# One-hots of a chunk as eight comparisons of 128 columns with a value per partition

## What is computed

```python
def gmm_conv(x, src, dst, edge_attr, g, mu, sigma, root_w, bias):      # K = 3 kernels
    diff = edge_attr[:, None, :] - mu[None, :, :]
    gauss = jnp.exp(jnp.sum(-0.5 * diff * diff / (EPS + sigma[None] ** 2), axis=-1))
    xj = x[src] @ g
    msg = jnp.einsum('eko,ek->eo', xj.reshape(E, K, OUT_DIM), gauss)
    summed = segment_sum(msg, dst)
    cnt = segment_sum(ones(E), dst)
    return summed / jnp.maximum(cnt, 1.0)[:, None] + x @ root_w + bias

x = layernorm(x + silu(gmm_conv(x, src, dst, ...) + x))
# two SAGE layers on the same edges: h @ W_self + mean_of_neighbours(h) @ W_neigh + b, relu between
x = layernorm(x + sage(relu(sage(x))))
```

## Time and profile before

| | us |
|---|---|
| median of 3 runs | 7659.32 (7652.49 to 7663.15) |
| the profiled execution's own time | 7651.4 |
| its span, first to last instruction | 7649.6 |
| DVE busy | 4374.6 (57%) |
| POOL busy | 3367.5 (44%) |
| PE busy | 5050.4 (66%) |
| L1329, 489 recorded, mean 1212 ns | 592.7 |

### The profile page before, as it was taken

The page is one execution under the profiler, slowest core; times in us unless marked ns, Lnnn a source line. Parts: engine busy times, 40 slices in busy tenths (PEclk is TensorE's granted clock), DMA queues, the critical chain, the costliest instruction groups (busy, mean ns, idle before and its releaser), DMA issues.

```text
span 7649.6 us, 144672 instructions
## 1 busy us (share of the span) xinstructions
PE 5050.4 (66%) x35195; PEld 4048.2 (53%) x35196; DVE 4374.6 (57%) x15088; ACT 2714.0 (35%) x8317; POOL 3367.5 (44%) x3146
## 2 busy tenths in 40 slices
PE   1565655555566666655555555555545899999999
PEld 1223333333344444444444444444425899999999
DVE  5668888767677777665656656566543322222222
ACT  3113333334444444455555555555532000000000
POOL 5024555555666666666666666666630000000000
PEclk9558888877788888777778888788775899999999
DMA  2001222212222222222222222222230799999998
GB/s 71 28 24 49 68 68 68 67 51 87 78 96 83 87 91 90 90 90 91 90 90 91 91 90 90 73 90 90 91 85 3 298 381 383 381 367 385 385 384 344
DMA packets 258352, 1082.32 MB, mean 141 GB/s; under 512 B 140102, under 2 KB 144230, under 8 KB 194406
## 3 DMA queue, kind: packets, MB, share of 16 engines
q1 hardware_dynamic: 142806, 968.66, 32.8%
q0 software_dynamic: 100352, 102.96, 6.9%
q10 hardware_dynamic: 14902, 8.11, 0.5%
HBM read 751.67 MB, written 327.81 MB: 141 GB/s over the span
## 4 chain that ended last, share of the span: by engine, by line
PE 39%; DVE 20%; issue 14%; DVEq 13%; POOL 5%; DMA 5%; ACT 4%; ACTq 1%; SPq 1%; POOLq 0%
PE pw L970 21%; PE pw L800 9%; DVE rE L1269 5%; POOL rE L512 5%; DVEq L1302 3%; DMA tab<-tab_d 3%; DVEq L1472 3%; PE pw L825 3%; DVE rE L1267 2%; DVE rE L1329 2%; PE pw L772 2%; ACT rE L559 1%; DVE rE L1395 1%; PE pw L937 1%; ACT sca L575 1%
## 5 line engine op out<-in xcount | busy, mean ns | idle before, releaser
L512 POOL DMA_INDIRECT rE<-in_x,idx x3136 | 3365.4, 1073 | 2262.7 <-issue 2092.9
L800 PE MATMUL pw<-rE 128*128 128x193 f32 x7824 | 1775.9, 391 | 921.5 <-DVE rE L1329 885.9
L598 ACT CAST rB<-pw 128x792 bf16<-128x792 f32 x1568 | 1259.6, 814 | 2903.6 <-PE pw L825 1489.4
L800 PEld LDWEIGHTS pw<-rE 128*128 128x128 f32 x7824 | 1623.7, 233 | 1130.5 <-DVE rE L1329 1061.5
L559 ACT ACTIVATE rE<-rE,cols 128x64 f32<-128x64 f32 x4704 | 1254.5, 344 | 8.2 <-DMA tab<-tab_d 8.2
L825 PE MATMUL pw<-rE 128*128 128x396 f16 x3840 | 804.1, 357 | 577.8 <-DVE rE L1269 576.8
L1269 DVE TENSOR_SCALAR rE<-iperm,gr 128x392 f16<-128x392 f16 x3840 | 1052.1, 314 | 0.0
L825 PEld LDWEIGHTS pw<-rE 128*128 128x128 f16 x3840 | 368.8, 103 | 954.4 <-DVE rE L1269 681.1
L970 PE MATMUL pw<-rB,rA 128*128 128x192 bf16 x9604 | 810.8, 246 | 0.1
L970 PE MATMUL pw<-rE,rA 128*128 128x192 bf16 x9604 | 810.4, 246 | 0.1
L970 PEld LDWEIGHTS pw<-rB,rA 128*128 128x128 bf16 x9604 | 790.8, 98 | 1.6
(11 more groups left out here) (256 smaller groups left out, 2626.6 us busy)
## 6 DMA issues: line engine op xcount, KB each, us to landing
rA<-count SPq DMA_DIRECT2D x392, 1568.0 KB, 8.5
count<-rB SPq DMA_DIRECT2D x98, 3136.0 KB
rE<-in_x,idx POOLq DMA_INDIRECT x3136
cols<-cols_d SPq DMA_DIRECT2D x98, 64.0 KB
cols_d<-rA SPq DMA_DIRECT2D x3, 1568.0 KB, 5.2
rA<-in_edge_attr ACTq DMA_DIRECT2D x1, 4608.0 KB
out<-gcol ACTq DMA_DIRECT2D x97, 32.0 KB, 5.8
count<-rB SPq DMA_DIRECT2D x8, 224.0 KB, 2.0
```

What stands on the lines that cost most here:

```text
L512: pool.indirect_dma_start(out=gath[:, s, u * CB + b, :], out_offset=None, in_=x, in_offset=bass.IndirectOffsetOnAxis(ap=idx[:, s, u * CB + ...
L598: act.copy(stage[:, s, :, j * 2 * W:(j + 1) * 2 * W].rearrange("p h (w n) -> p w h n", w=2), pu[j % 3][:, :, 0:CW].rearrange("p w (h n) -> ...
L800: ins = pe.matmul(sums[side][:, 0:AW], onehot[:, side, bb, :], wgath[:, side, bb, :], start=(bb == 0), stop=(bb == CB - 1))
```

## The change

The one instruction that writes the one-hots of all eight batches, comparing two operands of 128 x 1024 (the iota repeated for each batch, `local` repeated along the columns), becomes eight instructions. Each compares the 128 columns of `iota` with one column of `local`, taken as a value per partition. The last of the eight raises the semaphore. The bytes written, the waits and everything on the other engines are as before.

```diff
@@ -1326,9 +1326,9 @@
                     V.tensor_scalar(local[:], here[:, 0, :], tile128[:, bass.ds(tile, 1)], None, ALU.subtract).then_inc(a_loc, 1)
                     add_sums(k, side)
                     dve.wait_ge(a_loc, k)
-                    V.tensor_tensor(onehot[:, side], iota[:, None, :].broadcast_to([P, CB, P]),
-                                    local[:, :, None].broadcast_to([P, CB, P]),
-                                    ALU.is_equal).then_inc(a_oh[side], 1)
+                    for bb in range(CB):
+                        ins = V.tensor_scalar(onehot[:, side, bb, :], iota[:], local[:, bb:bb + 1], None, ALU.is_equal)
+                    ins.then_inc(a_oh[side], 1)
                     dve.reg_mov(prev[side], tile)
                     dve.reg_add(cs[side], cs[side], 1)
                     dve.reg_add(ck, ck, 1)
```

## The result

The changed kernel takes 7798.88 us (median of 4 runs, 7793.41 to 7800.85) against 7655.9 us for the kernel before (7649.76 to 7663.15 over 4): 1.0188 times as long, 95% interval 1.0176 to 1.0200, so 143 us more, where 170 were forecast. The profiled execution has a span of 7791.6 us, 142.0 more than before.

What follows compares the result with a forecast made beforehand. No engine bounds the whole; in the counting stage DVE is full early, then the consumers' chain, mostly DVE, leads. 55 + 50 + 18 + 16 + 31 = 170 us on 7651.4, plus 7.9, gave 7829 us, range 7715 to 7930.

Steps and rivals of the forecast that it cites:

- Removed and added: DVE, per one-hot set: 1.14 us removed, eight steps of 0.195 us (1.56) added, net +0.42 us.
- Holds by gathers: New comparisons on DVE lengthened by 0.11 us about once per POOL gather: 0.12 us more per set.
- 0 to 2144 us: First stretch of the counting stage, DVE without gaps: 110 sets at 0.50 us, 55 us.
- 2144 to 3200 us: Counting stage, consumers' chain nearly all DVE: 105 sets x 0.50 x 0.95, 50 us.
- 3200 us to the end: Later counting stage, to 5700 us, partly covered by waits: 18, 16 (halved from 33) and 31 us.
- The share of 0.6: From 3200 us, the part of DVE's increase taken to reach the time, the rest covered by waits.
- The lead: POOL's gathers ahead of preparations, 5.4 chunks at 2144 us, 2 at 4767: POOL slower, but consumers set their own time meanwhile.
- the shifts of 55 and 105 us: Sign of being right: preparation now at 2144 us comes 55 us later, and the shift is 105 by 3200.
- the step, ACT's waits and the shorter gathers: Signs of being right: comparisons start 0.19 to 0.20 us apart, ACT's row waits shrink, mean gather falls below 1073 ns.
- Rival 1: POOL's gathers, held less by short instructions, set the time from 2144 us on: 36 us faster, 7623 us; chance 6%.
- Rival 2: Second half covered by POOL and the table's DMA; only 50 to 75 us from the first half remain: 7722 us; 10%.
- Rival 3: Short instructions meet POOL far more often, 0.86 us more per set: +315 us, 7974 us; chance 8%.

Runs made afterwards that it cites:

- the mixed version: Kernel before, but from tile 16 on eight value-per-partition comparisons, each with its own signal, PE waiting batch by batch: 9259.56 us against 9043.57 (ratio 1.0247).

## Why the prediction was right

The direction and the size hold, and of the mechanism its larger part: 7798.88 us lies in the range of 7715 to 7930, 30 us below the value of 7829. By its steps:

- Removed and added. 0.195 us per step and 1.56 per set were forecast; 1.57 is read above. So the price of L1022's form was right, fixed part and column time together. DVE's busy time is up by 198.9 us, a little below the 210 to 260 given, or 0.41 per set where 0.50 was taken. The 0.11 us of gain by the fixed 58 cycles that the Trainium skill gives (VectorE: DVE Perf Modes, The TRN2 errata) did not come.
- Holds by gathers. 0.12 us per set were added for them. Without gathers the eight instructions are busy 811.5 us, with them 832.1: 20.6 / 489 = 0.04 us per set. This term was three times too high. Besides, the instructions of L1395 became shorter (546.0 us of busy time before, 527.1 after), which the sum had not counted.
- 0 to 2144 us. 55 us forecast, 33.5 measured. This is the term that was mis-sized most. "DVE at work without a gap around them" was true of L1329's surroundings and not of the tile: DVE's busy time rose by 48 us, and its idle time fell by 15. In kernels without POOL it is the same (35.8), so POOL is not the reason. Which waits gave room was not singled out by a run.
- 2144 to 3200 us. 50 forecast, 32.5 measured, for the same reason: 44 us more work, 12 less idle time.
- 3200 us to the end. 65 forecast, 76 measured. The share of 0.6 was too low: without POOL the stretch costs 174 - 69 = 105 us, 0.77 of the 274 x 0.50 = 137 that the prediction works with. A likely reason is that PE's later start, which the prediction named and then treated as part of the same 0.44 us, has a price of its own (0.11 us per set over the whole, and 46 of its 53 us come after tile 48).
- POOL. The lead was read rightly: up to tile 48 POOL costs nothing. In the later tiles it covers some 30 us, where the prediction had 16.

The first two errors were too high, the last too low, and they partly cancelled. That the total came within 27 us of the forecast is in part luck. Of the signs named for being right, the shifts of 55 and 105 us did not show (33.5 and 66.0) and DVE's busy time fell short; the step, ACT's waits and the shorter gathers did.

Rival 1 had its first half right: POOL was relieved, by 150 us of busy time, and nothing came of it in the time, because the consumers set the pace. Its forecast of 170 - 54 = 116 us holds a slip: 8 x 0.28 x 0.28 / 2 / 1.37 x 2/3 is 0.15 and not 0.11, so 75 us instead of 54, and 95 us of relief. Rival 2 would have had the shift stop at tile 26; it doubled by tile 48. Rival 3 is refuted by the 0.04 us per set. The rule of the Trainium skill (SBUF — State Buffer, Who interferes with whom) was read in the prediction as new holds for POOL under the one-input form and none under the two-input form. The traces show hardly any under the first (3 of the 406 gathers above take over 1.1 us) and long ones under the second. But the long ones do not contradict the page, as the prediction took them to. The same section says that an instruction with two SBUF inputs contends with a GpSimd instruction that reads SBUF, and a gather takes its indices from the tile `idx`. That this read is the cause was not tried.

## What to carry to other kernels

Splitting one instruction into n adds n - 1 fixed parts on its engine. Here eight pieces of 128 columns hold DVE 0.43 us longer than one of 1024, although a column costs about half. What it can bring back is an earlier start of the consumer. With a signal per piece PE can start about 1.4 us sooner (7 steps of 0.195, an estimate), and a change that lost 143 us wins 26. Before crediting an engine with a gain, count who leads: the lead between two chains told where POOL's gain could be seen in the time and where not.

## What was not expected of the hardware

- Two-operand f32 comparisons on DVE keep POOL's gathers out, one long one always (415 of 415), a row of short ones in over half of the cases (240 of 421); the mean gather is 1066 to 1075 ns with them. The same comparisons with a value per partition hardly do (12 of 406; mean gather 1025 ns, and 1016 in the mixed version).
- Eight comparisons of 128 columns hold DVE about as long in either form: the median step is 202 ns with two operands and 196 with a value per partition. So at this length the form saves next to nothing, though over many columns it has half the time per column.
- Where a one-operand comparison stands ahead of the two-operand one, the gathers are longer (1119 ns) than where it stands behind (1045). This was not followed up.
- Two chips took 9046 and 9044 us for the kernel for which a third takes 7652, with the same instructions. With seven of eight gathers left out one of them takes 7630. In the kernel with eight two-operand comparisons on such a chip ACT waits 1139 us for something that the trace does not record ("remote"). In the trace of the kernel before, on the first chip, there is no such wait.

```profile
ACT rB L598 <- remote: 1139.0, 167, 30.3
```

Since the forms with few gathers escape it, the landing of the gathers is the likely place; why it differs between chips is open.
